# First layer of a four-layer sequence kernel: row maxima made in slots 4 to 15 of the step ahead and slots 0 to 3 of the batch's own step

## The reference

```python
xt = jnp.transpose(x, (0, 2, 1))
q = xt @ Wq.T
qh = q.reshape(B, T, NH, dk).transpose(0, 2, 1, 3)
scores = scale * jnp.einsum('bhqd,bhkd->bhqk', qh, qh)
logits = (scores * cmask + (1.0 - cmask) * NEG) * rmask
attn = jax.nn.softmax(logits, axis=-1)
ctx = jnp.einsum('bhqk,bhkd->bhqd', attn, qh)
out = ctx.transpose(0, 2, 1, 3).reshape(B, T, D) @ Wo.T
...
x = x + _L0_cond_ref(x, cond_2048, L0_cond_Wq, L0_cond_Wo)
x = x + _L1_cond_ref(x, cond_2048[:, None, :])                       # depthwise convolution
x = x + _L2_cond_ref(cond_2048, x, L2_cond_W_ih, L2_cond_W_hh, ...)  # GRU over 256 steps
x = x + _L3_cond_ref(x, cond_2048, L3_cond_Wq, L3_cond_Wk, ...)      # attention, 16 heads
```

## Time and profile before

| | us |
|---|---|
| median of three runs | 2804.09 |
| lowest and highest run | 2798.7, 2814.0 |
| the profiled execution, its own time | 2816.45 |
| its span in the trace | 2814.6 |
| TensorE busy in the span | 2633.3 (94%) |
| DVE, ACT, POOL busy | 2097.5, 1348.0, 914.2 |
| first layer's steps 0 to 14 (first to last L660 of slot 0) | 51.8 to 705.3 |

### The profile page before, as it was taken

The page is one execution under the profiler, slowest core; times in us unless marked ns, Lnnn a source line. Parts: engine busy times, 40 slices in busy tenths (PEclk is TensorE's granted clock), DMA queues, the critical chain, the costliest instruction groups (busy, mean ns, idle before and its releaser), DMA issues. The chain is left out here.

```text
span 2814.6 us, 108219 instructions
## 1 busy us (share of the span) xinstructions
PE 2633.3 (94%) x46966; PEld 1503.7 (53%) x46966; DVE 2097.5 (75%) x4263; ACT 1348.0 (48%) x2344; POOL 914.2 (32%) x830
## 2 busy tenths in 40 slices
PE   8999999999989999999999999997999999999986
PEld 4333333333379898989999898983222222222221
DVE  5766666666788887888888887755777777777785
ACT  2555555555322222222322222211888787887876
POOL 1444444444022222222222222111244344344333
PEclk9999999999799999999999999998999999999999
DMA  2310111101100000000000000004344444544532
GB/s 66 94 55 28 54 37 46 55 28 43 27 14 0 0 0 0 0 0 0 0 0 0 0 0 0 0 5 108 74 107 116 107 106 112 114 104 112 115 91 52
DMA packets 120897, 132.05 MB, mean 47 GB/s; under 512 B 31800, under 2 KB 84944, under 8 KB 120674
## 3 DMA queue, kind: packets, MB, share of 16 engines
q1 hardware_dynamic: 114942, 123.12, 17.1%
q10 hardware_dynamic: 5760, 6.56, 0.8%
HBM read 85.29 MB, written 44.30 MB: 46 GB/s over the span
## 5 line engine op out<-in xcount | busy, mean ns | idle before, releaser
L912 PE MATMUL exp_ps<-region,gru_hT 128*16 128x128 f32 x16384 | 498.5, 274 | 39.3 <-DVE gru_hT L1039 7.8
L1582 DVE TENSOR_REDUCE x<-exp_ps 128x2 f32<-128x1024 f32 x352 | 426.0, 1221 | 104.8 <-PE exp_ps L1693 104.3
L912 PEld LDWEIGHTS exp_ps<-region,gru_hT 128*16 128x16 f32 x16384 | 428.3, 103 | 107.8 <-DVE gru_hT L1039 107.8
L845 POOL TENSOR_TENSOR xT<-xT,gru_hT 128x64 f32<-128x64 f32 x256 | 181.0, 707 | 824.6 <-DVE gru_hT L1039 815.6
L1508 ACT ACTIVATE region<-exp_ps,x 128x1024 f32<-128x1024 f32 x336 | 370.2, 1110 | 72.8 <-PE exp_ps L1664 72.8
L407 POOL TENSOR_TENSOR l_probs<-l_probs 128x1024 f32<-128x1024 f32 x120 | 281.1, 2349 | 297.7 <-ACT l_probs L483 220.1
L958 ACT ACTIVATE gru_r<-exp_ps 128x128 f32<-128x128 f32 x256 | 70.9, 277 | 588.1 <-PE exp_ps L912 588.1
L593 DVE TENSOR_REDUCE l_maxes<-exp_ps 128x2 f32<-128x1024 f32 x176 | 214.9, 1221 | 132.8 <-PE exp_ps L668 132.7
L997 DVE SCALAR_TENSOR_TENSOR xT<-x,condT,xT 128x512 f32<-128x512 f32 x420 | 311.0, 781 | 0.0
L897 PE MATMUL exp_ps<-region,gru_x_st 128*32 128x128 f32 x8192 | 272.1, 274 | 11.4 <-POOL gru_x_st L863 11.4
L1677 PE MATMUL bank<-region,x 128*17 128x512 f32 x2048 | 271.5, 602 | 6.7 <-ACT region L1508 3.6
(11 more groups left out here) (182 smaller groups left out, 4240.7 us busy)
## 6 DMA issues: line engine op xcount, KB each, us to landing
region<-key_query_scratch SPq DMA_DIRECT2D x128, 192.0 KB
key_query_scratch<-x SPq DMA_DIRECT2D x48, 256.0 KB, 2.5
key_query_scratch<-region SPq DMA_DIRECT2D x48, 256.0 KB, 2.5
region<-in_x SPq DMA_DIRECT2D x16, 512.0 KB, 4.8
l_xres<-in_x SPq DMA_DIRECT2D x16, 512.0 KB, 4.0
x_scratch<-x SPq DMA_DIRECT2D x16, 512.0 KB, 2.8
l_rden<-rden_scratch SPq DMA_DIRECT2D x120, 64.0 KB, 2.1
l_rden<-rden_scratch SPq DMA_DIRECT2D x240, 32.0 KB, 1.8
```

The costliest lines, as they stand in the source:

```text
L845: pool.tensor_tensor(dst, dst, hT[:, q, :, HALF:QW], ALU.add).then_inc(added, 1)
L912: last = pe.matmul(out[QW * j:QW * j + rows, cols], hT[:, p, k, state], group_of(wh[:, k, gate, :], j), start=False, stop=True, skip_group ...
L1582: dve.tensor_reduce(maxes[:, half, qt, head % HH:head % HH + 2], pairs[ring.place[2 * slot + 1]][:, :, :], AX_X, ALU.max).then_inc(taken[" ...
```

## The change

Two things are moved, and nothing is added to or taken from what is computed.

First, the 16 maxima tiles of a batch. `tile_at(slot)` returns tile (slot - 4) modulo 16: slots 4 to 15 of the step ahead hold tiles 0 to 11, and slots 0 to 3 of the batch's own step hold tiles 12 to 15. The first half's split now falls in slot 11 of the step ahead and the second half's in slot 3 of the batch's own step.

Second, the table: "mtb" from slot 1 to 5, "v1" from 5 to 6, "mta" from 10 to 13, "v0" from 13 to 14. "q1", "q0", "out", the reciprocal and the sums stay. GpSimd's `step` is the same as before.

```diff
-    AT = {"mtb": 1, "q1": 3, "v1": 5, "mta": 10, "q0": 11, "v0": 13, "out": 15, "reciprocal": 5, "sums": 10}
+    AT = {"mtb": 5, "q1": 3, "v1": 6, "mta": 13, "q0": 11, "v0": 14, "out": 15, "reciprocal": 5, "sums": 10}
+    FIRST = 4
...
+        def tile_at(slot):
+            return (slot - FIRST) % SLOTS, 0 if slot < FIRST else 1
...
-            order += [(slot, "st", slot, 0, 16), (slot, "max", slot, 1, 16)]
+            order += [(slot, "st", slot, 0, 16), (slot, "max", *tile_at(slot), 16)]
...
-                    if active(s, 1):
-                        half, qt, hp = max_tile(slot)
-                        wait(dve, ready["max"], 16 * (s + 1) + slot + 1)
+                    tile, ahead = tile_at(slot)
+                    if active(s, ahead):
+                        half, qt, hp = max_tile(tile)
+                        wait(dve, ready["max"], 16 * (s + ahead) + tile + 1)
...
-                        if slot % 8 == 7:
-                            split(half, "mtb" if half else "mta", s + 1)
+                        if tile % 8 == 7:
+                            split(half, "mtb" if half else "mta", s + ahead)
...
-                if active(s, 1):
-                    if slot % 8 == 0:
-                        wait(pe, kq_done[half], s + 2)
+                if active(s, ahead):
+                    if tile % 8 == 0:
+                        wait(pe, kq_done[half], s + ahead + 1)
                     tasks.free(pe, s, at["max"])
+                    of = (par + ahead) % 2
```

More of the change, by code:

```diff
@@ L301, in l0_part, with max_tile @@
         block = ctx.enter_context(nc.Block())
-        def max_tile(slot):
-            return slot // 8, slot % 8 // 2, 1 - slot % 2
+        def max_tile(tile):
+            return tile // 8, tile % 8 // 2, 1 - tile % 2
         @block.sync
@@ L586, in step @@
                 for slot in range(SLOTS):
-                    if active(s, 1):
-                        half, qt, hp = max_tile(slot)
-                        wait(dve, ready["max"], 16 * (s + 1) + slot + 1)
-                        if slot % 8 == 0:
-                            wait(dve, split_done, 2 * s + half + 1)
-                        dve.tensor_reduce(maxes[:, half, qt, 2 * hp:2 * hp + 2], tasks.bank_of("max", slot)[:, :, :], AX_X, ALU.max)\
+                    tile, ahead = tile_at(slot)
[3 more added lines that the diff above has]
+                        if tile % 8 == 0:
+                            wait(dve, split_done, 2 * (s + ahead - 1) + half + 1)
+                        dve.tensor_reduce(maxes[:, half, qt, 2 * hp:2 * hp + 2], tasks.bank_of("max", tile)[:, :, :], AX_X, ALU.max)\
                            .then_inc(taken["max"], 1)
-                        if slot % 8 == 7:
-                            split(half, "mtb" if half else "mta", s + 1)
+                        if tile % 8 == 7:
+                            split(half, "mtb" if half else "mta", s + ahead)
                     for kind, idx, off in (("q1", 1, 1), ("q0", 0, 2)):
@@ L650, in products @@
                 grp, kt = seg // 4, seg % 4
-                half, qt, mp = max_tile(slot)
-                at = {kind: next(n for n, t in enumerate(tasks.tasks) if t[1] == kind and t[2] == slot) for kind in ("st", "max")}
+                tile, ahead = tile_at(slot)
+                half, qt, mp = max_tile(tile)
+                at = {kind: next(n for n, t in enumerate(tasks.tasks) if t[0] == slot and t[1] == kind) for kind in ("st", "max")}
                 if active(s, 0):
@@ L661, in products @@
                                   max_rows[row:row + NPART, grp, :], start=True, stop=False)
-                if active(s, 1):
-                    if slot % 8 == 0:
-                        wait(pe, kq_done[half], s + 2)
+                if active(s, ahead):
+                    if tile % 8 == 0:
+                        wait(pe, kq_done[half], s + ahead + 1)
                     tasks.free(pe, s, at["max"])
+                    of = (par + ahead) % 2
                     for i in range(2):
                         rows = slice(QW * (2 * mp + i), QW * (2 * mp + i) + QW)
-                        last = pe.matmul(tasks.bank(at["max"])[:, i, :], kq[rows, 1 - par, half, qt * P:qt * P + P],
-                                         kq[rows, 1 - par, half, :], start=True, stop=True)
+                        last = pe.matmul(tasks.bank(at["max"])[:, i, :], kq[rows, of, half, qt * P:qt * P + P],
+                                         kq[rows, of, half, :], start=True, stop=True)
                     last.then_inc(ready["max"], 1)
```

## The result

The changed kernel takes 2919.5 us (median of 4 runs, 2917.1 to 2923.4) against 2803.8 for the kernel before (also 4 runs, 2798.7 to 2814.0): a ratio of 1.0409, 95% interval 1.0378 to 1.0441, 115.7 us slower. Forecast were 2925 and a range of 2885 to 2990. The profiled executions differ by less, 2915.3 against 2814.6 us of span (+100.7), as that of before lies 12 us above its median. The page of the kernel after answers to the earlier trace rows: TensorE busy for 14 us more, a smaller share of a longer span.

The account below looks back on a forecast made before the run. The prediction took TensorE, busy 94% of the span with an in-order queue, to bound the kernel. Its terms, 76 + 21 + 27 - 4 + 1 = +121 us, gave 2925 us against 2804.09, range 2885 to 2990.

Parts of the forecast that it names:

- A: Slot 5: TensorE idles behind "mtb" for POOL's column and two additions, 5.1 us a step, 76 us.
- B: Slot 11: the first half's split is held by POOL's additions, delaying "mta" and slot 14; 1.4 a step, 21 us.
- C: TensorE behind slot 5's hole: half clock for 3.6 us after the restart, 1.8 us a step, 27 us.
- D, step -1: Step -1: four maxima tiles go, 1.06 us each, -4 us.
- D, last step: Last step: four maxima tiles come, with four reductions and a split on DVE; bounds 0 and 6, taken as +1 us.
- Rival 3: Slot 5: POOL's additions are in time, so no hole; +18, 2822 us; chance 0.04.
- Rival 1: Behind slot 5's hole: TensorE's clock does not fall; +94, 2898 us; chance 0.14.
- rival 2: Behind slot 5's hole: clock stays low much longer, 12 us of half clock a step; 2988 us; chance 0.16.
- one sign of being wrong: TensorE's clock: the prediction is wrong if more than 6 us a step are spent at half clock.
- rival 4: Steps -1 and last: faster, as moved tiles keep the last step's clock high (-12); 2788 us; chance 0.06.

Follow-up runs that it names:

- the filler: Changed kernel with 14 identity products on TensorE between the turn "mtb" and the denominators of slot 5, into a bank overwritten afterwards: 2904.5 us, ratio 1.036.
- the turn alone: Kernel before with only the turn "mtb" moved from slot 1 to slot 5, the maxima tiles left in place: 2916.0 us, ratio 1.0403.
- The first experiment: Changed kernel with POOL's mask column that waits for "mtb" moved behind the step's first two additions: 2828.7 us, ratio 1.0099.
- the fifth: Changed kernel with the column behind the first two additions, each split one reduction later, maskings in slots 5 and 14, second scaling in slot 13: 2794.1 us, ratio 0.9958.
- the second experiment: Changed kernel with POOL's mask column placed between the step's first two additions: 2865.8 us, ratio 1.022.
- The seventh experiment: Kernel before with four more maxima products in slots 0 to 3 of the last step, whose results nothing reads: 2801.9 us, ratio 0.9991.

## Why the prediction was right, and where it was not

| Term | predicted | measured in the first layer |
|---|---|---|
| A, hole of slot 5 | 76 | 75.0 (15 of 5.00) |
| B, split in slot 11 | 21 | 14.1 + some 0.3 x 15 = 18.5; the 0.3 is what a filled step (50.0) has over 43.77 + 5.00 + 0.94 |
| C, half clock behind the hole | 27 | (8.32 - 5.00 - 0.94 - 0.29) x 15 = 31; 26 by the filler's 15 steps as they were |
| D, step -1 | -4 | -5.1 (first product of step 0: 46.66 against 51.76) |
| D, last step | +1 | -9.9 (45.20 against 55.11) |
| Sum | +121 | +109.5; the layer's own row says +108.4 |

**A** came as worked out: the rows above have it link by link, and it took no more than moving the column behind the additions to remove it. Rival 3 (additions in time) is excluded, and the turn alone shows that "mtb" in slot 5 is enough to make the kernel 4% slower.

**B** came with a wait of 0.94 where 1.05 was worked out. The first experiment showed that each split which the additions hold, with the turn's reduction behind it, costs such a wait, and the fifth that a split clear of them costs none. The second one, in slot 3, comes only once the hole is closed; the prediction was right to price the split there at 0.20 for this kernel. In the earlier trace rows the held cast cost nothing: the turn stood in slot 10, three slots behind the split, and by then DVE had caught up (it idles 1.23 us ahead of slot 11's reduction). The Trainium skill (SBUF — State Buffer, "Who interferes with whom") says that VectorE's two-port copies and casts and GpSimd share one pair of ports, and whoever issues first has it for the whole instruction. The traces agree: 2.37 us for the cast beside an addition, 0.19 to 0.20 without, and 4.72 / 2 = 2.36 for one addition.

**C** was right in its kind and at most 4 us too low. The filler products took 2.1 us from every step behind whose hole they kept the clock up, and left the waits as they were, so the half clock is the cause and not some other delay behind the hole. Rival 1 (the clock does not fall) is excluded by the windows, and rival 2 (12 us of half clock or more) also: the clock was back 4.5 us after the restart, somewhat later than the 3 to 4 us of the prediction. Of this term the row at the earlier trace rows was the better guide, and not that of the last step. By its letter one sign of being wrong did come: more than 6 us a step at half clock were seen, 6.8 in 12 of the 15. Of these, 2.3 us lie in the wait, where they cost nothing, and 4.5 are paid. The shorter hole of the second experiment lies between the earlier trace rows's 1.12 us (never) and 5.0 (always): 5 times in 15.

**D, the last step,** is the term with the largest miss. I counted the work that comes (four tiles, four reductions) and put it at +1. The profile says -9.9: the step got shorter, because its granted clock rose from 0.73 to 0.93. That is the mechanism of rival 4, with -12 as its price; I had tied it to "if neither A nor B comes", though nothing in A or B stands in its way. The mechanism was not exclusive with the forecast, only too small to turn it.

Its size in an ordinary run is smaller, as far as the record goes. The seventh experiment, which makes this change alone, shows -10 in the profile and -2.5 in the medians. And the profiled execution of before, from which the 55.11 us are read, lies 12.6 us above its median. Some 4.5 to 8.5 of these are in the part behind the first layer, where it alone takes 2027.9 us and the nine others 2019.4 to 2023.3. That leaves 4 to 8 us for the first layer, and if all of it is the last step's low clock, an ordinary last step is shorter by 2 to 6 us in the changed kernel and not by 9.9. This is an estimate from these rows; no profile of a median run of before shows it. With -2.5 for the term all terms sum to +117, near the +115.7 of the medians; that fits, but shows nothing.

The forecast was thus 5 us from the median, with B too high by 2.5 us, the last step too high by some 3 to 7 and C too low by up to 4. That these partly cancel is luck; that A, the largest term, came within 1 us is not.

**The better version.** The idea of the change (maxima in their own step, fewer tiles in step -1, more in the last) is worth 0.4% when two things are mended: no column that waits for "mtb" ahead of additions that the next product needs, and no split beside POOL's additions. The version with both runs at 2794.1 us, ratio 0.9942 to 0.9975.

## What to carry over

Before moving an item later on one engine, list what waits for it on the others, and what stands behind each waiter in its own queue: here 0.25 us of work cost 5 us a step because two additions were queued behind it. Price a hole on TensorE as its length plus half of the time at half clock behind the restart, taken from a restart in the same trace, and look for waits that the hole keeps off and that come when it is closed. And count a thin stretch at low clock as a place where added products can cost nothing.

## What was unexpected

- A last step with TensorE busy for 53.26 of 57 us has a granted clock of 0.73, and with four more pairs of products 0.93 (42.25 busy of 46). Being busy by the profile did not keep the clock.
- Step -1 ran at half clock for all of its last 20 us in one of the ten profiles (0.51; 1.00 in the kernel after) and for some 7 us in two, with nothing in the code ahead of it to tell them apart from the others. It cost 9.2 us of the first layer in the one and 3.4 in the two, a part of what repeated runs of one kernel scatter by.
- A hole of 2.7 us lowered the clock in 5 of 15 steps of one execution, and one of 5.0 us with all but 1.84 filled in 1 of 15, though the steps are alike.
